# Low parts of the first node table between the copies of the node sums, and the first adjacency loads ahead of the store of these sums

## The reference, cut to what matters

```python
edge_index = jnp.stack([src, dst])
x = _layernorm(x + L0(x, edge_attr_128, src, dst, ...))
x = _layernorm(x + L1(x, edge_index, ...))
x = _layernorm(x + L2(x, edge_index, ...))
x = _layernorm(x + L3(x, edge_index, edge_attr_16, ...))
# L0: agg = segment_sum(edge_attr, receivers); relu([agg, nodes] @ W1 + b1) @ W2 + b2
# L1: agg = segment_sum(x[src], dst); h = (1 + eps) * x + agg; two matmuls, each with a norm over all nodes
# L2: two mean aggregations segment_sum(x[src], dst) / cnt, each with matmuls
# L3: deg = segment_sum(1, col); loop_attr = segment_sum(edge_attr, col) / max(deg, 1); attention over edges
```

## Time and profile before

| | us |
|---|---|
| median of 3 runs | 3255.97 (3255.94 to 3266.86) |
| the profiled execution | 3259.57 |
| its span, first to last instruction | 3258.0 |
| TensorE matmuls busy | 2375.3 (73%) |
| VectorE busy | 1558.1 (48%) |
| GpSimd busy | 1420.6 (44%) |
| ScalarE busy | 695.3 (21%) |

### The profile page before, as it was taken

One profiled execution on the slowest core, in us unless ns is written; L12 is line 12 of the kernel. 1 busy time (PEld: TensorE's weight loads), 2 busy tenths in 40 slices (PEclk: granted clock), 3 DMA queues, 4 the chain that ended last, 5 costly groups with the idle time before them and its releaser, 6 DMA issues. The chain is left out here.

```text
span 3258.0 us, 68630 instructions
## 1 busy us (share of the span) xinstructions
PE 2375.3 (73%) x21724; PEld 2088.1 (64%) x21725; DVE 1558.1 (48%) x3763; ACT 695.3 (21%) x1091; POOL 1420.6 (44%) x1498
## 2 busy tenths in 40 slices
PE   3799899899899945999889982566530104999965
PEld 2677777787788724888778872566520104989954
DVE  5676667533211273111143337888879002545567
ACT  0187778555000141000010000000000100000043
POOL 4522212123000031122224447777778777767665
PEclk9999999999899967999989996777865555555577
DMA  5589899823788627888789985989862534655511
GB/s 159 144 271 293 277 285 292 282 70 97 247 284 283 195 56 251 251 248 247 222 258 288 295 226 151 192 186 190 188 150 72 168 107 126 148 144 144 140 35 43
DMA packets 560774, 627.41 MB, mean 193 GB/s; under 512 B 265887, under 2 KB 412524, under 8 KB 560041
## 3 DMA queue, kind: packets, MB, share of 16 engines
q1 hardware_dynamic: 258425, 387.60, 39.7%
q10 hardware_dynamic: 252072, 164.25, 19.1%
q0 software_dynamic: 50208, 74.70, 9.5%
HBM read 484.61 MB, written 142.11 MB: 192 GB/s over the span
## 5 line engine op out<-in xcount | busy, mean ns | idle before, releaser
L895 POOL DMA_INDIRECT rows<-x_rows,src_i x832 | 849.5, 1021 | 281.3 <-issue 234.3
L1585 PE MATMUL ps<-slices,wide 128*128 128x250 f16 x7350 | 826.7, 270 | 48.1 <-DMA slices<-adjacency 48.1
L1585 PEld LDWEIGHTS ps<-slices,wide 128*128 128x128 f16 x7350 | 714.6, 98 | 135.8 <-issue 28.3
L1828 PE MATMUL ps<-slices 128*128 128x75 bf16 x4992 | 242.2, 224 | 165.8 <-DVE slices L2627 165.8
L1828 PEld LDWEIGHTS ps<-slices 128*128 128x128 bf16 x4992 | 235.8, 116 | 172.3 <-issue 172.3
L930 POOL TENSOR_TENSOR ea_one<-ea,ones 128x64 f32<-128x64 f32 x250 | 127.4, 511 | 420.4 <-DMA ea<-in_edge_attr 396.7
L1525 PE MATMUL ps<-weighted,slices 128*128 128x57 f32 x1120 | 253.6, 418 | 69.3 <-DVE weighted L2204 69.3
L1525 PEld LDWEIGHTS ps<-weighted,slices 128*128 128x128 f32 x1120 | 247.2, 333 | 69.9 <-DVE weighted L2204 69.6
L1464 PE MATMUL ps<-rows,weighted 128*32 128x128 f32 x2000 | 277.3, 284 | 11.6 <-DMA ea<-in_edge_attr 9.1
L1525 PE MATMUL ps<-weighted,rows 128*128 128x57 f32 x544 | 130.6, 419 | 190.0 <-DMA rows<-x_rows,src_i 165.3
L1525 PEld LDWEIGHTS ps<-weighted,rows 128*128 128x128 f32 x544 | 123.4, 332 | 192.8 <-issue 165.5
(11 more groups left out here) (356 smaller groups left out, 3425.4 us busy)
## 6 DMA issues: line engine op xcount, KB each, us to landing
slices<-adjacency SPq DMA_DIRECT2D x525, 437.5 KB, 5.4
rows<-in_edge_attr SPq DMA_DIRECT2D x250, 256.0 KB
adjacency<-wide ACTq DMA_DIRECT2D x91, 437.5 KB, 4.1
adjacency<-slices ACTq DMA_DIRECT2D x84, 437.5 KB, 3.8
x_of_edges<-rows SPq DMA_DIRECT2D x140, 256.0 KB
slices<-x_of_edges ACTq DMA_DIRECT2D x140, 256.0 KB
slices<-src_low ACTq DMA_DIRECT2D x52, 512.0 KB
rows<-x_rows,src_i POOLq DMA_INDIRECT x832
```

Of the source, the lines that this page charges most:

```text
L895: pool.indirect_dma_start(out=packed[i][:, c, :], out_offset=None, in_=table, in_offset=bass.IndirectOffsetOnAxis(ap=rows_of, axis=0)).the ...
L1585: mm = pe.matmul(ps_d[b], high_low[:, part, QS * s + q, :], slices[:, s, PN * q:PN * (q + 1)], start=(s == 0 and q == 0 and part == 0), st ...
L1828: mm = pe.matmul(ps_g[:, s, b, c, 0:HEADS * QH], lowT[:, s, b, h, P * c:P * (c + 1)], tab_b[:, n, h, :, :].rearrange("p h i -> p (h i)"), ...
```

## The change

On VectorE, the code of one low part becomes a function, and the low parts of table 0 no longer come behind all copies: behind copies 6 to 12 stands one low part each. `low_parts(1)` and `low_parts(2)` are as before. On SP, the loads of block 0 no longer stand behind the store of the sums: the store comes behind them and behind the rows' load. The wait for the store's landing and the load of `cntB` move into block 1, between the load of its part 1 and that of its part 2.

```diff
                 def body(q, u, b, first):
                     for s in range(SL):
+                        if k == 0 and isinstance(q, int) and q == 1 and s == 2:
+                            sp.wait_ge(sums_out, 16)
+                            sp.dma_start(cntB[:, :, :], sums_d.rearrange("k (j p) -> j k p", p=TN)).then_inc(sums_in, 16)
                         if isinstance(q, int) and q == 0:
                             sp.wait_ge(low_ready, SL * k + s + 1)
...
                     if k == 0 and isinstance(q, int) and q == 0:
-                        sp.wait_ge(sums_out, 16)
-                        sp.dma_start(cntB[:, :, :], sums_d.rearrange("k (j p) -> j k p", p=TN)).then_inc(sums_in, 16)
+                        sp.wait_ge(node_sums, 1 + PIECES)
+                        sp.dma_start(sums_d, nsum[0:1 + HEADS, 0:N]).then_inc(sums_out, 16)
                 pairs(sp, body)
...
             load_table(0, x1_d, d0)
-            sp.wait_ge(node_sums, 1 + PIECES)
-            sp.dma_start(sums_d, nsum[0:1 + HEADS, 0:N]).then_inc(sums_out, 16)
             load_dense(0, x1_d, d1a, d1a.T)
...
+            def low_part(k, s):
+
+                v.wait_ge(high_ready, SL * k + s + 1)
+                v.scalar_tensor_tensor(high_low[:, 1, QS * s:QS * (s + 1), :]...,
+                                       table[:, s, 0:QS * P], scale[:, 0:1], ...,
+                                       ALU.mult, ALU.subtract).then_inc(low_ready, 1)
             def low_parts(k):
                 v.wait_ge(scaled, SCALED[k])
                 for s in range(SL):
-                    v.wait_ge(high_ready, SL * k + s + 1)
-                    v.scalar_tensor_tensor(...).then_inc(low_ready, 1)
+                    low_part(k, s)
...
             for k in range(PIECES):
                 v.wait_ge(sums_pe, k + 1)
                 at = slice(512 * k, min(512 * (k + 1), N))
                 v.tensor_copy(nsum[0:1 + HEADS, at], ps[1 + k % SUM_BANKS][...]).then_inc(node_sums, 1)
+                if k >= PIECES - SL:
+                    if k == PIECES - SL:
+                        v.wait_ge(scaled, SCALED[0])
+                    low_part(0, k - PIECES + SL)
             uncovered_rows(0)
-            low_parts(0)
```

More of the change, by code:

```diff
@@ L2329, in scale_parts @@
                 v.tensor_copy(scale[:, :], ps_m[:, P:P + 2]).then_inc(scaled, 1)
+            def low_part(k, s):
+                v.wait_ge(high_ready, SL * k + s + 1)
+                v.scalar_tensor_tensor(high_low[:, 1, QS * s:QS * (s + 1), :].rearrange("p q f -> p (q f)"),
+                                       table[:, s, 0:QS * P], scale[:, 0:1],
+                                       high_low[:, 0, QS * s:QS * (s + 1), :].rearrange("p q f -> p (q f)"),
+                                       ALU.mult, ALU.subtract).then_inc(low_ready, 1)
             def low_parts(k):
```

## The result

The changed kernel takes 3252.77 us (median of 15 runs, 3244.5 to 3262.65), the kernel before 3260.33 us (15 runs, 3254.93 to 3270.46). The ratio is 0.9977, with a 95% interval of 0.9967 to 0.9988: 7.5 us less, between 3.9 and 10.8. Forecast were 6.9 us less. The absolute time is 3.7 us over the forecast because the median before, from three runs at first, moved up by 4.4 us with twelve more. Taken alone, 3252.77 us lies nearest to the 3252.4 of case 2, and the interval of the gain reaches from just above case 2's 3.55 us to beyond case 5's 8.2. So the times say only that the kernel became faster; which case came is read from the traces.

What follows compares the result with a forecast made beforehand. TensorE was taken as the bound, idle in a hole before the first adjacency load lands. 7.25 us gained less 0.4 given back makes 6.9, from a median of 3255.97 to 3249.1 us (chance 0.62), range 3244.5 to 3256.

Steps and rivals of the forecast that it cites:

- case 2: Rival, chance 0.17: the store holds its four engines longer, TensorE stalls 3.7 us in block 1; gain 3.55, 3252.4 us.
- case 5: Rival, chance 0.10: TensorE's clock rises at once in the dense part; gain 8.2, 3247.8 us.
- Step 1: VectorE's low parts between the copies: a pair costs 1.66 us in a period of 1.71, so slip 0.
- The bound without overlap: Upper bound for VectorE's copy and low part: 1.83 us a pair, slipping 0.12 in six periods, 0.7 us in all.
- Step 2: Block 0's loads go out with the low parts; TensorE's dense part starts at 822.84 instead of 830.09, gain 7.25 us.
- Step 3: TensorE's clock in block 0: the low stretch costs 1.3 us as before, so no change; bounds 1.3 gained, 0.7 lost.
- The same again: Clock rise in block 0 taken as before: the low stretch costs 84 dense matmuls 1.3 us again.
- the bound of 0.7 us on the side of the loss: Block 0's clock: a rise after 4 us instead of 2.6 costs 0.7 us more.
- Step 4: Store of the sums behind block 0's loads on SP: block 1's load 2 comes late, costing 0.4 us; bounds 0 and 3.7.
- The give-back: Loss in block 1: load 2 lands at 839.1, needed at 838.7, 0.4 us; bounds 0 and 3.7.
- case 3: Rival, chance 0.05: SP stands at the store's landing in block 1, TensorE behind it; 3256.6 us, or 3265.6 with 20 us packets.
- case 4: Rival, chance 0.06: TensorE starts the dense part late for another reason, at 4 us; gain 3.9, 3252.1 us.

Runs made afterwards that it cites:

- the low parts alone: Against the changed kernel, SP's queue put back as before (store of the sums ahead of block 0's loads): first add 41.8 us, first dense matmul 29.0 us.
- the queue's order alone: Against the changed kernel, VectorE's low parts put back behind all copies: first dense matmul 26.7 us, first add 39.9 us behind the first matmul of the sums.

## Why the prediction was right

**What bounds it.** Right: the hole was the gain ("the low parts alone" and "the queue's order alone" show that it needs both edits), TensorE was the bound behind it, and the shift of the first add (7.58 us) is that of the last dense matmul (7.6) and of the first gather (7.8).

**Step 1.** Right to a tenth. Low part 5 hands over to the short copy after 1.06 us (818.40 to 819.46), as computed, where the paced ones take 1.10 (809.87 to 810.97), so the pair fitted the period with 0.04 us to spare. The copies didn't slip, and the last low part ends at 820.77, where the forecast of 825.0 less 4.12 says 820.9. The bound without overlap was not needed.

**Step 2.** Load 0 was issued at 811.02, forecast 815.2 - 4.12 = 811.1, and landed after 3.2 us. The term for TensorE's passage through semaphore and branch was mis-sized: 0.61 us were taken from VectorE's row, none shows on TensorE. The dense part starts at 818.04, as the last piece ends (797.12 + 20.99 = 818.11). So 7.93 us instead of 7.25.

**Step 3.** "The same again" was off by 0.35 us in this execution: 84 dense matmuls from 818.04 to 828.70 take 10.66 us instead of 10.31, and block 0 12.58 us up to its add instead of 12.2, which the prediction had named as the sign that this step is wrong. In the other traces with the parts of block 0 back to back it was 10.91 to 11.64 us, and 10.91 and 11.26 of them where the hole stood as before or nearly. So the trace before had the earliest rise of all, 2.7 us behind the first dense matmul (read as 2.6 in the prediction), and the bound of 0.7 us on the side of the loss was too narrow by 0.6. Why the rise comes earlier or later stays open. Case 5 (a rise at once) is refuted.

**Step 4.** That SP's wait and the loads on either side of it are the place of the price is right, as the moved wait and the doubled store showed. How the store gets through was wrong in two terms, and they cancelled by luck. Shifted by the 4.12 us, its packets were to start at 824.4 and to take 3.6 us each; by the packet records they start at 826.07, 826.22, 826.59 and 826.97 and take 1.06 to 1.11 us each. So it waited 4.5 us behind the loads, which is most of the 7.0 us from issue to landing (forecast 6.1), and landed at 828.5 where 827.9 was forecast. The 3.6 us is what the four packets take when they start on an idle queue, as in the trace before and with the low parts alone. In the six traces where the store stands once behind the loads on SP's queue they took 0.93 to 1.70 us; only with the store made twice did some of the eight take up to 3.95. The landings of block 1's loads 0, 1 and 2:

```profile
L777 SPq DMA_DIRECT2D slices<-adjacency x1: 357/357/357, 822.3 to 822.3; - x1
DMA to landing us min/median/max: 7.3/7.3/7.3
L777 SPq DMA_DIRECT2D slices<-adjacency x1: 1201/1201/1201, 822.9 to 822.9; - x1
DMA to landing us min/median/max: 8.2/8.2/8.2
L777 SPq DMA_DIRECT2D slices<-adjacency x1: 349/349/349, 828.9 to 828.9; - x1
DMA to landing us min/median/max: 4.0/4.0/4.0
```

Load 2 came faster than the 6.6 us that I took from the crowded stretch before: while SP stands, the DMA share falls to 0.45 and 0.27 (827 to 829 us). It landed at 832.9, 1.4 us before it was wanted (834.27). Loads 0 and 1 each landed 0.8 us before use, where 1.6 and 1.8 were forecast; this is the place where the change is nearest to a price. How much of their 7.3 and 8.2 us is the store's isn't shown: in the kernel before the same two loads took 7.9 and 7.5 us without it. The give-back is 0 and not 0.4 us. Cases 2, 3 and 4 did not come: no wait for a load stands in block 1, and TensorE starts at once.

**The sum.** 7.25 - 0.4 = 6.9 forecast; 7.93 - 0.35 = 7.58 in the trace; 7.5 in the timed runs. The errors of the terms, +0.68, -0.35 and +0.4, left 0.7 between them, and inside step 4 two larger ones had cancelled. So the hit within 0.7 us is better than the working deserves.

## What to carry to other kernels

When an engine idles ahead of a transfer, look at what the transfer's own queue stands behind as well as at what produces its data: here either edit alone gave 0 and 2.2 us, both gave 7.9. Work of another engine fits into a paced loop for nothing if the hand-over times (start to start, not durations) fit into the period. A transfer that is late for nobody can still delay its neighbours: place its wait behind loads that don't need it, here two of them. A duration read on an idle queue need not hold on a busy one: the store's packets took 3.6 us there and 1.1 here, and the landing was right only because the time they waited in the queue was too short in the working.

## What the runs showed of the hardware

The store of four rows of 25,000 bytes keeps four DMA engines for 3.6 us each when it starts on an idle queue, that is 100 KB in 3.6 us or 27 GB/s for the four together, where the loads of the adjacency reach 357 GB/s on 16. Its packets take as long with the low parts alone (3.63 to 3.71 us), but 1.06 to 1.11 us in the changed kernel, where they start behind the loads, and on ScalarE's queue 1.70 to 3.51 us. With the rows in separate DMAs they went one after the other, 0.93 to 1.09 us each (27 GB/s for one row alone at 0.93), and the end came only 0.9 us later. So four rows at once on an idle queue moved no more than one row at a time, while in the changed kernel all four passed between 826.07 and 828.02 us, 51 GB/s. What sets these rates the runs don't show.

SP's issue of the rows' load took 3.61, 2.15 and 2.12 us instead of 0.34 while a store from ScalarE's queue was under way (three traces); one issue of 2.01 us without such a store says that there are other reasons as well.

The rise of the clock behind the first dense matmul took 2.7 us before, 3.4 in the changed kernel's first trace, 3.5 to 5.4 in eight of the others, 5.9 and 7.7 us in the two versions with the sums inside block 0, with the same dense matmuls. TensorE was busy throughout the 21 us of the sums ahead of them, at 0.50.
